# TensorE's side work in single pieces, one buffer each for delta and du, a ring of 12 slots, and a new order at the end of a batch

## The chip, the cores and the metric

The program runs on one core of a Trainium2 chip. The metric is the time of one execution on the device, in microseconds (us). All times below are in us unless marked ns. The engines are TensorE (PE, with its weight loads as PEld), VectorE (DVE), ScalarE (ACT), GpSimd (POOL) and SyncE (SP, which issues DMAs).

## The reference, cut to what matters

```python
# attention-like block: a selective state-space model; B=4, L=512, DM=256, DI=512, DS=16
x     = einsum('ed,bld->bel', in_proj_w, ctx)            # in_proj
u     = silu(causal_depthwise_conv(x, conv_w) + conv_b)
x_dbl = einsum('ke,bel->bkl', x_proj_w, u)               # 16 rows dt_lo, 16 rows B, 16 rows C
delta = softplus(einsum('er,brl->bel', dt_proj_w, dt_lo) + dt_proj_b)
A     = -exp(A_log)                                      # 512 x 16
state = state * exp(delta_t * A) + (delta_t * u_t) * B_t # for t in 0..511, 16 states per channel
y_t   = sum_n state * C_t
out   = (y + D * u) * silu(layernorm(x_in))              # added to x_in
# then, on layernorm(x): 8 experts of 512 -> 1024 -> 512, top 2 per token
gate_logits = einsum('bsd,de->bse', xln, gate_kernel)
```

## The kernel before

The program has two stages one after the other: `mamba_block` (the state-space part for four batches, ending with the gate logits) and `ffn_block` (the experts). The change touches only the first.

**Tiling.** A batch b (0 to 3) has 512 channels by 512 times, in two halves of 256 channels. For each half the 16 states n are worked through one by one; one state of one half is a *unit*, q = 32 b + s, with s = 0 to 31 the step in the batch. A unit holds 128 partitions by 1024 values and lives in one slot of `ring`. It passes through five operations:

- POOL `times_b` (L284): du times the broadcast row B, into the ring slot. POOL's code issues it four units (LEAD) ahead of its other work. It may not start before `acc` has emptied the slot, RING = 8 units back.
- ACT `exp_dA` (L368): two exponentials of 512, into three PSUM banks (SB = 3). It can therefore be three half units ahead of the scan, no more.
- DVE `scan` (L588): two scans of 512 along time.
- `times_c`: states times the broadcast row C. For n in (2, 5, 8, 11, 14) POOL does it (L293), from a DMA'd row; for the others DVE does it (L594) one step later than the scan, and the row comes from PE: `fill_c` (L733) writes the single PSUM bank Cb, and may only do so when the DVE product before it is done.
- PE `acc` (L753): 8 transposes that add the unit into yT, two units (LAG) later.

**Side work.** Between the units the engines prepare batch b + 1 and finish batch b - 1. Each engine's block is a loop over s with `if s == ...` lines, written out by hand, and each engine runs its own list in order. In order of use, for the next batch: PE `ctx_T`, `in_proj` (L772); ACT `tap`, DVE `conv` (L604), ACT `silu_u`; PE `x_proj` (L782), ACT `x_dbl` (L358), PE `dt_proj` (L790), ACT `dt_half` (L420, L421) and `soft` (L448, L452), DVE `loss` (L611), POOL `sub_loss` (L299), ACT `soft_log` (L456), POOL `add_ln` and `times_u` (L313), which gives the `du` that `times_b` needs. dt, `loss` and the rest are done in halves: half 0 of batch b + 1 in the second half of batch b, half 1 partly in batch b + 1. For the batch before: PE `zs_T` (of this batch's gate), DVE `drain_y` (L620), `stats_2`, POOL `rstd_2`, ACT `xln`, PE and ACT `gate_T`, PE `logits_of` (L814) and DVE `logit_copy` (L625). PE's side results go through two PSUM banks pp0 and pp1 in the order of the list USES. `logit_copy(b - 1)` stands after the loop over s, so DVE reaches it at the end of each of the batches 1 and 2, and for batch 3 after the last product.

## Time and profile before

| | us |
|---|---|
| median of 3 runs (lowest, highest) | 1291.56 (1291.31, 1293.41) |
| the profiled execution's own time | 1293.37 |
| its span in the trace | 1290.7 |
| PE busy | 1117.9 |
| DVE busy | 755.9 |
| POOL busy | 639.3 |
| ACT busy | 524.3 |

The first scan starts at 40.57 and the last product of the state-space part, `drain_y` of batch 3's second half, at 544.38; the rest of the span is its short tail and the experts, where PE is the chain. The first stage is where several engines pass small pieces to each other; busy shares over the whole span mix the two.

### The profile page before, as it was taken

The numbers are of one execution on the slowest core, as the hardware profiler recorded it, in microseconds if no ns is written. First come the engines' busy times: TensorE is split into PE (matmuls) and PEld (weight loads), VectorE is DVE, ScalarE is ACT, GpSimd is POOL, SyncE is SP. The second block draws the span as 40 slices with busy tenths as digits, with TensorE's granted clock in tenths as the row PEclk, the third lists the DMA queues.
The fourth block names the chain that finished last, engine by engine and source line by source line (L and its number), as shares of the span: only waits on it lengthen the run. The fifth ranks groups of instructions, "written<-read, shape, count | busy, mean of one in ns | idle before, by whom it ended". The sixth has DMA issues, their size and how long they took to land.

```text
span 1290.7 us, 19382 instructions
## 1 busy us (share of the span) xinstructions
PE 1117.9 (87%) x4940; PEld 836.3 (65%) x4940; DVE 755.9 (59%) x823; ACT 524.3 (41%) x706; POOL 639.3 (50%) x465
## 2 busy tenths in 40 slices
PE   6677778797788767738999999999999999999994
PEld 2344454465456545637788888888888888888883
DVE  5888999979987989656324343531532534324321
ACT  5955756665566554213223132421422323213210
POOL 0798999999989899304122232221321223212221
PEclk9677888878877767657999999999999999999997
DMA  6432232522432233064214353421531435215310
GB/s 208 142 104 92 84 112 76 174 85 87 129 110 90 82 112 109 0 250 174 99 41 164 106 179 113 165 105 43 179 104 35 171 108 179 105 41 171 106 47 19
DMA packets 65444, 145.08 MB, mean 112 GB/s; under 512 B 8654, under 2 KB 11214, under 8 KB 65408
## 3 DMA queue, kind: packets, MB, share of 16 engines
q1 hardware_dynamic: 56368, 116.34, 26.8%
q0 software_dynamic: 9040, 28.32, 6.7%
q8 instruction: 16, 0.26, 0.1%
q14 instruction: 20, 0.16, 0.0%
HBM read 320.53 MB, written 18.35 MB: 263 GB/s over the span
## 4 chain that ended last, share of the span: by engine, by line
PE 53%; DVE 2%; issue 0%; ACT 0%; POOL 0%; ACTq 0%; DVEq 0%; POOLq 0%
PE hp L1507 11%; PE hp L1506 11%; PE hp L1505 11%; PE yp L1505 5%; PE yp L1507 5%; PE yp L1506 5%; PE tp L1546 2%; PE xp L1499 1%; PE yp L1551 0%; DVE R L1343 0%; DVE S_tok L1339 0%; DVE S_w L1334 0%; DVE S_w L1447 0%; DVE S_w L1445 0%; DVE xT_lo L1402 0%
## 5 line engine op out<-in xcount | busy, mean ns | idle before, releaser
L284 POOL TENSOR_TENSOR ring<-du,bB 128x1024 f32<-128x1024 f32 x128 | 299.9, 2361 | 53.2 <-DVE du L654 36.7
L588 DVE TENSOR_TENSOR_SCAN ring<-dA,ring 128x512 f32<-128x512 f32 x256 | 296.0, 1205 | 15.4 <-ACT dA L368 9.9
L368 ACT ACTIVATE dA<-delta,Acol 128x512 f32<-128x512 f32 x256 | 172.3, 687 | 165.4 <-DVE ring L588 162.7
L1505 PE MATMUL hp<-w_hi,xT_hi 128*128 128x512 f32 x592 | 236.5, 399 | 2.1 <-DVE xT_lo L1402 2.1
L1507 PE MATMUL hp<-w_hi,xT_lo 128*128 128x512 f32 x592 | 236.2, 399 | 0.0
L1506 PE MATMUL hp<-w_lo,xT_hi 128*128 128x512 f32 x592 | 234.1, 396 | 0.0
L753 PEld LDWEIGHTS yT<-ident,ring 128*128 128x128 f32 x1024 | 146.7, 172 | 93.3 <-issue 76.2
L733 PE MATMUL Cb<-xdbl,ident 48*128 48x512 f32 x176 | 125.9, 802 | 91.8 <-DVE ring L594 91.8
L1144 POOL COPY out_index<-out_tab 128x1 uint32 x37 | 6.7, 181 | 356.5 <-DVE work L1409 356.5
L1423 DVE TENSOR_TENSOR work<-hp,work 128x512 f32<-128x512 f32 x74 | 51.1, 690 | 224.3 <-PE hp L1507 221.1
L753 PE MATMUL yT<-ident,ring 128*128 128x128 f32 x1024 | 172.8, 331 | 8.0 <-POOL ring L293 8.0
L1380 DVE TENSOR_TENSOR w_lo<-stage,w_hi 128x2048 fp32r<-128x2048 f32 x48 | 109.0, 2289 | 35.6 <-ACT w_hi L1190 35.4
L1505 PEld LDWEIGHTS hp<-w_hi,xT_hi 128*128 128x128 f32 x592 | 111.7, 189 | 28.0 <-DVE xT_lo L1402 1.8
L1506 PEld LDWEIGHTS hp<-w_lo,xT_hi 128*128 128x128 f32 x592 | 111.7, 189 | 26.9
L1507 PEld LDWEIGHTS hp<-w_hi,xT_lo 128*128 128x128 f32 x592 | 111.5, 188 | 26.1
L1505 PE MATMUL yp<-w_hi,iT_hi 128*128 128x512 f32 x296 | 121.8, 412 | 2.1 <-DVE iT_lo L1434 2.1
L594 DVE TENSOR_TENSOR ring<-Cb,ring 128x1024 f32<-128x1024 f32 x88 | 106.4, 1209 | 24.4 <-PE Cb L733 23.3
L1229 ACT CAST iT_hi<-tp 128x512 fp32r<-128x512 f32 x74 | 39.8, 590 | 194.5 <-PE tp L1546 194.5
L1507 PE MATMUL yp<-w_hi,iT_lo 128*128 128x512 f32 x296 | 117.3, 396 | 0.0
L1506 PE MATMUL yp<-w_lo,iT_hi 128*128 128x512 f32 x296 | 116.7, 394 | 0.0
L1409 DVE SCALAR_TENSOR_TENSOR work<-yp,wtab,work 128x512 f32<-128x512 f32 x37 | 27.8, 751 | 145.0 <-PE yp L1507 145.0
L733 PEld LDWEIGHTS Cb<-xdbl,ident 48*128 48x128 f32 x176 | 32.4, 229 | 122.1 <-DVE ring L594 66.8
(202 smaller groups left out, 1403.4 us busy)
## 6 DMA issues: line engine op xcount, KB each, us to landing
stage<-in_L_ffn_w_kernel_dram SPq DMA_DIRECT2D x160, 1024.0 KB
stage<-in_L_ffn_wo_kernel_dram SPq DMA_DIRECT2D x78, 1024.0 KB
bB<-bcs SPq DMA_DIRECT2D x64, 512.0 KB, 3.6
bC<-bcs SPq DMA_DIRECT2D x40, 256.0 KB, 4.4
xall<-in_x_dram SPq DMA_DIRECT2D x1, 4096.0 KB, 14.1
xln_dram<-xlnb SPq DMA_DIRECT2D x4, 1024.0 KB, 6.8
out_dram<-xall SPq DMA_DIRECT2D x4, 1024.0 KB, 8.9
ctx_rows<-in_ctx_dram SPq DMA_DIRECT2D x4, 512.0 KB, 6.0
```

The source lines that it names most:

```text
L284: g_.tensor_tensor(ring[:, q % RING, :].rearrange("p (e l) -> p e l", e=2), dub(b, h * 2 * L, 2 * L).rearrange("p (e l) -> p e l", e=2), B ...
L368: a_.activation(dA[r % SB][:, :], db(b, eb * L, L), ACT.Exp, scale=Acol[:, eb, n:n + 1]).then_inc(exp_done, 1)
L588: v_.tensor_tensor_scan(o, dA[r % SB][:, :], o, 0.0, ALU.mult, ALU.add).then_inc(scan_done, 1)
L594: v_.tensor_tensor(states, Cb[:, :].unsqueeze(1).to_broadcast([P, 2, L]), states, ALU.mult).then_inc(hc_dve, 1)
L733: t_.matmul(Cb[:, :], ident[0:rows, at:at + 1].to_broadcast([rows, P]), xdbl[:, b % 2, :], start=True, stop=True).then_inc(C_full, 1)
L753: last = t_.matmul(yT[:, t, e * P:(e + 1) * P], ring[:, q % RING, e * L + t * P:e * L + (t + 1) * P], ident[:, :], start=False, stop=(n == ...
L1229: s_.copy(iT_hi[:, 4 * h:4 * h + 4, :], tp[h][:, :].rearrange("p (k t) -> p k t", t=P)).then_inc(i_hi, 1)
L1380: v.tensor_tensor(w_lo[c][:, :, :], stage[c][:, :, :], w_hi[c][:, :, :].bitcast(fp32), ALU.subtract).then_inc(lo_done, 1)
L1423: v.tensor_tensor(inter[:, h, :], hp[2 + h][:, :], gated[:, h, :], ALU.mult).then_inc(inter_done, 1)
L1505: t_.matmul(bank[:, :], a_hi[:, k, :], b_hi[:, b, :], start=(start and k == ks[0]), stop=False)
L1506: t_.matmul(bank[:, :], a_hi[:, k, :], b_lo[:, b, :], start=False, stop=False)
L1507: last = t_.matmul(bank[:, :], a_lo[:, k, :], b_hi[:, b, :], start=False, stop=(stop and k == ks[-1]))
```

## The change

Five things are altered, none of which adds or removes an arithmetic instruction:

1. PE's side work is cut so that at most one piece (one bank of `ctx_T`, `zs_T`, `in_proj` or `gate_T`, half of `x_proj`, half of the logits) stands between two units.
2. `delta` and `du` have one buffer instead of two, so `dt_half` now waits for the exponentials and `times_u` of the batch before, and `loss` for the `times_b` of the batch before.
3. The ring has 12 slots instead of 8.
4. `dt_half(b + 1, 0)` and `soft` move from ACT's step 24 to 23 and `soft_log` from 27 to 26; PE's `dt_proj(b + 1, 0)` moves from 21 to 22.
5. `gate_T` of rows 2 and 3, the logits and `logit_copy` move ahead of `dt_proj(b + 1, 1)` and `dt_half(b + 1, 1)`: PE's gate from step 28 to 23 and 24, ACT's from 31 to 25, the logits from 31 to 26 and 27, DVE's copy from behind the loop to step 29, PE's second half of dt from 25 to 30, ACT's from 28 to 31.

```diff
--- before.py
+++ after.py
@@ -8,7 +8,7 @@
-RING = 8
+RING = 12
...
-        delta = sb("delta", [P, 2, EB * L])
-        du = sb("du", [P, 2, EB * L])
+        delta = sb("delta", [P, EB * L])
+        du = sb("du", [P, EB * L])
...
-            USES += [f"{n}.{b + 1}" for n in ("XP", "DT0", "DT1", "DT2", "DT3") if nxt]
+            USES += [f"{n}.{b + 1}" for n in ("XP", "DT0", "DT1") if nxt]
             USES += [f"{n}.{b - 1}" for n in ("G2", "G3", "LG") if rest]
+            USES += [f"{n}.{b + 1}" for n in ("DT2", "DT3") if nxt]
...
-                if b > 1:
-                    act.wait_ge(du_ready, g - 3)
+                if b > 0:
+                    act.wait_ge(du_ready, g - 1)
+                    act.wait_ge(exp_done, 2 * (q0(b - 1, i) + UPH))
...
                     if s == 21 and nxt:
                         x_dbl(b + 1)
-                    if s == 24 and nxt:
+                    if s == 23 and nxt:
                         dt_half(b + 1, 0)
                         soft(b + 1, 0)
-                    if s == 27 and nxt:
-                        soft_log(b + 1, 0)
-                    if s == 28 and nxt:
-                        dt_half(b + 1, 1)
-                    if s == 31 and rest:
+                    if s == 25 and rest:
                         gate_T(b - 1, 2)
                         gate_T(b - 1, 3)
+                    if s == 26 and nxt:
+                        soft_log(b + 1, 0)
+                    if s == 31 and nxt:
+                        dt_half(b + 1, 1)
...
-                if b > 1:
-                    dve.wait_ge(dbu_done, q0(b - 2, i) + UPH)
+                if b > 0:
+                    dve.wait_ge(dbu_done, q0(b - 1, i) + UPH)
...
                         loss(b + 1, 0)
-                if rest and nxt:
-                    logit_copy(b - 1)
+                    if s == 29 and rest:
+                        logit_copy(b - 1)
             if NU - 1 in NTH_DVE:
                 times_c(NU - 1)
-            logit_copy(NB - 2)
             drain_y(NB - 1, 1)
...
-            def x_proj(b):
+            def x_proj(b, ebs):
                 o, done = use(f"XP.{b}")
                 if b > 0:
                     pe.wait_ge(u_ready, b)
-                for eb in range(EB):
+                for eb in ebs:
                     if b == 0:
                         pe.wait_ge(u_part, eb + 1)
                     last = t_.matmul(o[0:DR + 2 * DS, :], xpT[:, eb, :], ub(b, eb * L, L), start=(eb == 0), stop=(eb == EB - 1))
-                last.then_inc(done, 1)
+                if eb == EB - 1:
+                    last.then_inc(done, 1)
...
-            def logits_of(b):
+            def logits_of(b, rows):
                 for i in (LB - 2, LB - 1):
                     k = USE[f"G{i}.{b}"]
                     pe.wait_ge(freed[k % 2], nth(k))
                 o, done = use(f"LG.{b}")
-                for i in range(LB):
+                for i in rows:
                     for d in range(DI // P):
                         last = t_.matmul(o[:, i * 8:(i + 1) * 8], gT[:, i, d * P:(d + 1) * P], gate[:, d, :], start=(d == 0), stop=(d == DI // P - 1))
-                last.then_inc(done, 1)
+                if i == LB - 1:
+                    last.then_inc(done, 1)
...
-                    if s == 0 and nxt:
-                        ctx_T(b + 1)
-                    if s == 3 and rest:
-                        zs_T(b, (0, 1))
-                    if s == 6 and rest:
-                        zs_T(b, (2, 3))
-                    if s == 4 and nxt and not rest:
-                        in_proj(b + 1, (0, 1))
-                    if s == 8 and nxt and rest:
-                        in_proj(b + 1, (0, 1))
-                    if s == 9 and not rest:
-                        zs_T(b, (0, 1))
-                    if s == 11 and not rest:
-                        zs_T(b, (2, 3))
-                    if s == 12 and nxt:
-                        in_proj(b + 1, (2, 3))
-                    if s == 16 and rest:
-                        gate_T(b - 1, 0)
-                        gate_T(b - 1, 1)
+                    if s in (0, 1) and nxt:
+                        ctx_T(b + 1, (s,))
+                    if s in (4, 5, 7, 8) and rest:
+                        zs_T(b, ((4, 5, 7, 8).index(s),))
+                    if s in (9, 10, 11, 12) and not rest:
+                        zs_T(b, (s - 9,))
+                    if s in ((9, 10) if rest else (4, 5)) and nxt:
+                        in_proj(b + 1, (s - (9 if rest else 4),))
+                    if s in (13, 14) and nxt:
+                        in_proj(b + 1, (s - 11,))
+                    if s in (16, 17) and rest:
+                        gate_T(b - 1, s - 16)
                     if s == 19 and nxt:
-                        x_proj(b + 1)
-                    if s == 21 and nxt:
+                        x_proj(b + 1, (0, 1))
+                    if s == 20 and nxt:
+                        x_proj(b + 1, (2, 3))
+                    if s == 22 and nxt:
                         dt_proj(b + 1, 0)
-                    if s == 25 and nxt:
+                    if s in (23, 24) and rest:
+                        gate_T(b - 1, s - 21)
+                    if s == 26 and rest:
+                        logits_of(b - 1, (0, 1))
+                    if s == 27 and rest:
+                        logits_of(b - 1, (2, 3))
+                    if s == 30 and nxt:
                         dt_proj(b + 1, 1)
-                    if s == 28 and rest:
-                        gate_T(b - 1, 2)
-                        gate_T(b - 1, 3)
-                    if s == 31 and rest:
-                        logits_of(b - 1)
```

The first place is PE around `x_proj` and `dt_proj` in the first of the batches that have all side work (batch 1, steps 18 to 23; u, xpT are `x_proj`, dtT is `dt_proj`, xlnb is the gate). Before:

```order
L733 MATMUL Cb<-xdbl,ident 128x512
L753 MATMUL yT<-ident,ring 128x128 x8
L782 MATMUL pp<-u,xpT 48x512 x4
L733 MATMUL Cb<-xdbl,ident 128x512
L753 MATMUL yT<-ident,ring 128x128 x16
L790 MATMUL pp<-xdbl,dtT 128x512 x2
L733 MATMUL Cb<-xdbl,ident 128x512
L753 MATMUL yT<-ident,ring 128x128 x8
```

and now:

```order
L734 MATMUL Cb<-xdbl,ident 128x512
L754 MATMUL yT<-ident,ring 128x128 x8
L783 MATMUL pp<-u,xpT 48x512 x2
L734 MATMUL Cb<-xdbl,ident 128x512
L754 MATMUL yT<-ident,ring 128x128 x8
L783 MATMUL pp<-u,xpT 48x512 x2
L754 MATMUL yT<-ident,ring 128x128 x8
L734 MATMUL Cb<-xdbl,ident 128x512
L754 MATMUL yT<-ident,ring 128x128 x8
L792 MATMUL pp<-xdbl,dtT 128x512 x2
L734 MATMUL Cb<-xdbl,ident 128x512
L754 MATMUL yT<-ident,ring 128x128 x8
```

The second half of `x_proj` now stands behind one more Cb fill and one more `acc`, and `dt_proj` behind another pair.

The second place is ACT in the same stretch (steps 21 to 28 and on). xdbl is `x_dbl`, the four with spy and delta are `dt_half`, the next two `soft`, dA are the exponentials of the units. Before:

```order
L358 ACTIVATE xdbl<-pp 48x512
L368 ACTIVATE dA<-delta,Acol 128x512 x6
L420 ACTIVATE spy<-pp,dtb 128x512
L421 ACTIVATE delta<-pp,dtb 128x512
L420 ACTIVATE spy<-pp,dtb 128x512
L421 ACTIVATE delta<-pp,dtb 128x512
L448 ACTIVATE spy<-spy 128x1024
L452 ACTIVATE spw<-spy 128x1024
L368 ACTIVATE dA<-delta,Acol 128x512 x6
L456 ACT_TABLE_LOAD
```

and now:

```order
L359 ACTIVATE xdbl<-pp 48x512
L369 ACTIVATE dA<-delta,Acol 128x512 x4
L422 ACTIVATE spy<-pp,dtb 128x512
L423 ACTIVATE delta<-pp,dtb 128x512
L422 ACTIVATE spy<-pp,dtb 128x512
L423 ACTIVATE delta<-pp,dtb 128x512
L450 ACTIVATE spy<-spy 128x1024
L454 ACTIVATE spw<-spy 128x1024
L369 ACTIVATE dA<-delta,Acol 128x512 x4
L359 ACTIVATE gT<-pp 128x512 x2
L369 ACTIVATE dA<-delta,Acol 128x512 x2
L458 ACT_TABLE_LOAD
```

There are four exponentials (two units) instead of six between `x_dbl` and `dt_half`.

The third place is DVE at the end of batch 1, from the product of unit 28 on. Before:

```order
L594 TENSOR_TENSOR ring<-Cb,ring 128x1024
L588 SCALAR_TENSOR_TENSOR ring<-dA,ring 128x512 x2
L594 TENSOR_TENSOR ring<-Cb,ring 128x1024
L588 SCALAR_TENSOR_TENSOR ring<-dA,ring 128x512 x2
L625 COPY logits<-pp 128x32
L588 SCALAR_TENSOR_TENSOR ring<-dA,ring 128x512 x2
```

and now:

```order
L596 TENSOR_TENSOR ring<-Cb,ring 128x1024
L627 COPY logits<-pp 128x32
L590 SCALAR_TENSOR_TENSOR ring<-dA,ring 128x512 x2
L596 TENSOR_TENSOR ring<-Cb,ring 128x1024
L590 SCALAR_TENSOR_TENSOR ring<-dA,ring 128x512 x4
```

The copy of the logits has moved two units forward.

## Rows read from the trace of the kernel before

**Rows 1.** Windows, batches 1 and 3: length, busy PE, PEld, DVE, ACT, POOL, clock, DMA, GB/s

```profile
163.47:291.23 127.76, 102.41 (x445) 65.57 (x444) 114.96 (x112) 80.32 (x114) 123.97 (x59) 0.81 0.37 114
...
418.97:533.64 114.67, 86.74 (x363) 57.61 (x364) 104.92 (x99) 58.33 (x84) 103.32 (x51) 0.72 0.26 85
```

**Rows 2.** DVE's waits from 40 to 545: waiter <- releaser: us in total, times, longest

```profile
DVE ring L594 <- PE Cb L733: 23.3, 17, 2.5
DVE logits L625 <- PE pp L814: 19.1, 3, 7.2
```

**Rows 3.** Timeline of DVE, batch 1, steps 22 to 31: start, us, what, [idle before]

```profile
253.15 4.56 DVE L588 TENSOR_TENSOR_SCAN ring<-dA,ring 128x512 f32<-128x512 f32 x4
...
258.73 2.33 DVE L588 TENSOR_TENSOR_SCAN ring<-dA,ring 128x512 f32<-128x512 f32 x2
...
262.65 2.34 DVE L588 TENSOR_TENSOR_SCAN ring<-dA,ring 128x512 f32<-128x512 f32 x2 [0.38 <-ACT dA L368]
264.91 1.20 DVE L611 SCALAR_TENSOR_TENSOR du<-spw,spy 128x1024 f32<-128x1024 f32 x1
...
291.12 0.19 DVE L625 COPY logits<-pp 128x32 f32<-128x32 f32 x1 [5.81 <-PE pp L814]
```

**Rows 4.** Timeline of PE, batch 1, steps 19 to 24

```profile
245.13 1.12 PE L733 MATMUL Cb<-xdbl,ident 48*128 48x512 f32 x2
246.19 1.09 PE L753 MATMUL yT<-ident,ring 128*128 128x128 f32 x8
247.21 3.63 PE L782 MATMUL pp<-u,xpT 128*48 128x512 f32 x8
...
253.72 1.98 PE L790 MATMUL pp<-xdbl,dtT 16*128 16x512 f32 x4
...
258.87 2.07 PE L733 MATMUL Cb<-xdbl,ident 48*128 48x512 f32 x2 [1.09 <-DVE ring L594]
```

**Rows 5.** Timeline of ACT, batch 1, steps 21 to 24

```profile
250.88 0.59 ACT L358 ACTIVATE xdbl<-pp 48x512 f32<-48x512 f32 x1 [3.50 <-PE pp L782]
...
257.25 0.67 ACT L420 ACTIVATE spy<-pp,dtb 128x512 f32<-128x512 f32 x1
...
261.88 2.72 ACT L368 ACTIVATE dA<-delta,Acol 128x512 f32<-128x512 f32 x4
```

**Rows 6.** Timeline of POOL, batch 1, from `sub_loss` to the next first `times_b`

```profile
266.19 2.35 POOL L299 TENSOR_TENSOR delta<-delta,du 128x1024 f32<-128x1024 f32 x1 [2.27 <-DVE du L611]
...
282.57 2.35 POOL L284 TENSOR_TENSOR ring<-du,bB 128x1024 f32<-128x1024 f32 x1
```

**Rows 7.** Timeline of DVE, batch 1, the second `conv`

```profile
225.83 4.01 DVE L604 SCALAR_TENSOR_TENSOR u<-pp,convw,u 128x511 f32<-128x511 f32 x6
```

**Rows 8.** The end of batch 3: timelines of DVE and of PE

```profile
540.87 0.19 DVE L625 COPY logits<-pp 128x32 f32<-128x32 f32 x1 [7.23 <-PE pp L814]
544.38 1.22 DVE L620 TENSOR_TENSOR g<-yT,zsT 128x1024 f32<-128x1024 f32 x1 [3.31 <-PE yT L753]
...
534.00 6.83 PE L814 MATMUL pp<-gate,gT 128*128 128x8 f32 x32
540.69 3.65 PE L753 MATMUL yT<-ident,ring 128*128 128x128 f32 x16
```

**Rows 9.** One line, L611 (`loss`): ns min/median/max, and first and last start

```profile
L611 DVE SCALAR_TENSOR_TENSOR du<-spw,spy x8: 1199/1200/3377, 32.4 to 433.8; 128x1024 f32<-128x1024 f32 x8
```

**Rows 10.** Timelines of DVE and POOL, batch 1, step 3, the long `loss`; POOL's waits on ring slots

```profile
179.34 3.38 DVE L611 SCALAR_TENSOR_TENSOR du<-spw,spy 128x1024 f32<-128x1024 f32 x1
...
179.28 2.35 POOL L293 TENSOR_TENSOR ring<-ring,bC 128x1024 f32<-128x1024 f32 x1
181.59 5.63 POOL L284 TENSOR_TENSOR ring<-du,bB 128x1024 f32<-128x1024 f32 x2
...
POOL ring L284 <- PE yT L753: 16.0, 9, 3.5
```

**Rows 11.** Timeline of ACT, batch 1, step 13, `xln`, which waits for POOL's `rstd_2`

```profile
216.61 2.93 ACT L480 ACTIVATE xlnb<-xall,nm,rs 128x512 f32<-128x512 f32 x4 [0.41 <-POOL nm L264]
```

12 lines of the change are left out of this document (6 added, 6 removed).

## The prediction

> **What bounds the kernel now.** I read the windows by batch first. Batch 1 lasts 127.76 with DVE busy 114.96 and POOL 123.97, and batch 3 114.67 with DVE 104.92 [rows 1]: no engine is idle for long, so what counts is how far each runs ahead of the next. DVE is where the units come together, so I read its waits next: 23.3 for Cb in 17 waits, 19.1 for the logits in 3 [rows 2]. The logits' waits are 5.81 at the end of batch 1 [rows 3], 7.23 at the end of batch 3 [rows 8], and so 6.1 for batch 2. Then the timelines around the moved pieces. The reader is to see in them that ACT is fed by PE just in time: `x_dbl` starts at 250.88 after a wait of 3.50 for `x_proj` [rows 5], which ends at 250.84 [rows 4], and the scan of unit 22 starts at 253.15 [rows 3], about 1.1 after its exponential, whose 0.69 ends near 252.1. What comes later on PE than now reaches DVE almost in full, because only three half units of exponentials can be ready.
>
> **Units of cost.** At 2.4 GHz a Cb fill takes 1.1 and an `acc` 1.1 (1.12 and 1.09); half of `x_proj` is 1.8 (half of 3.63) and a `dt_proj` bank 1.0 (half of 1.98) [rows 4]. At 1.2 GHz a fill takes 2.07 [rows 4] and an `acc` 1.8 (half of 3.65) [rows 8]. A scan pair is 2.25 (4.56 for two pairs) [rows 3]; a DVE product adds 1.1, taken from the same spacing. The logits of a batch take 6.83 [rows 8], so a half is 3.4, or about 2.6 where the clock is high (an estimate from the fill's ratio, softened because their cost is weight loads).
>
> **Term 1: x_proj in halves, dt half 0 one unit earlier on ACT: +3.3 in each of batches 0, 1, 2, so +9.9.** In batch 1 the first half ends at 249.0; the fill of unit 20 waits for the product before it (about 248.9) and ends at 250.1, `acc` at 251.2, and the second half at 253.0 instead of 250.84. `x_dbl` (0.59) and the exponential (0.69) follow: scan 22 at 254.4, not 253.15, though the Cb wait before it is gone. Then PE does `acc`, fill, `acc` (3.3) and the first dt bank: 257.3. ACT needs from the start of `dt_half` to the end of the next exponential 257.25 to 261.88, and 0.69: 5.3 [rows 5]. So the exponential of unit 24 is there at 262.6, while DVE wants it at 254.4 + 4.5 + 1.1 = 260.1: it idles 2.5. Now scan 24 starts at 258.73 and scan 25, after one more product, at 262.65 with 0.38 idle [rows 3]. After the change scan 25 starts at 262.6 + 2.25 + 1.1 = 266.0: 3.3 late. Bounds: 0 if all of it hides, 9 if the clock is low (fills, `acc` and matmuls double, +5.7).
>
> **Term 2: the end of batches 1 and 2: -1.7 and -2.0.** From the end of `loss` (266.11) to scan 0 of the next batch (291.23) it is 25.1 now [rows 3]. POOL's own chain from `loss` to its next `times_b`, 266.19 to 284.92, is 18.7 [rows 6], a floor. With both logits halves in front of the fill of unit 28, and `dt_proj` behind `acc(28)`, PE's work after the product of unit 25 is fill, acc, half, acc, half, fill, acc, fill, acc, acc, two dt banks: at 2.4 GHz about 16, then ACT's two last operations and an exponential (2.1), and 3.4 from `loss` to that product: 21.2 to 21.5. The other way to it is from now's own run: there PE got through its list, logits last, at 291.1. The new list in front of dt lacks the last unit's fill and `acc` (2.2) and the gate (1.0), has the two dt banks (2.0) and idles about 1.5 less, so it ends near 288.4, and 2.1 behind that the exponential is 24.4 after `loss`. Between 21.5 and 24.4, both from rows, I take 23.4, nearer to the second because the granted clock was 0.81 there, some 40% of the time at the low level [rows 1]. So not 5.8 and 6.1 come back but 1.7 and 2.0; bounds -3.8 and, with the whole list at 1.2 GHz (26 instead of 16), +6 each. What is late next is `dt_half(b + 1, 1)`, behind which the next batch's exponentials are queued.
>
> **Term 3: batch 0's end, +1.1.** No logits there, but `dt_proj(1)` waits on PE behind `acc(27)`, which waits for POOL's `times_c`; in POOL's chain [rows 6] that is 14 after `loss`, so dt arrives at 18.1 and the exponential at 20.2, against 19.1 now (25.1 - 5.8 - 0.2 of batch 1, which is alike).
>
> **Term 4: in_proj banks 2 and 3 a unit later, +2.7.** After the product of unit 12 PE needs fill, acc, 1.8, acc, 1.8 = 6.9, and ACT's tap 0.8: 7.7. `conv` (at 225.83 now [rows 7]) wants that bank 6.3 after the product: +1.4 in batches 1 and 2, 0 in batch 0, where a Cb wait of about the same size goes. Bounds 0 and 3.5 each.
>
> **Term 5: the first halves, +2.0.** `zs_T` and the first `in_proj` banks also come one or two units later to ACT. In batch 1 POOL covers this: scan 14 needs `xln` (at 216.61, waiting for POOL's `rstd_2` [rows 11]), and POOL is busy all the time. In batch 2, where POOL now starts ahead thanks to the logits wait, I count 2.0, bounds 0 and 5.
>
> **Term 6: gate_T in halves, -2.1.** It shortens one Cb wait in each of batches 1 and 2, mean wait 23.3/17 = 1.4 [rows 2]; 0 to -2.8, and I take -2.1.
>
> **Term 7: ring of 12, single buffers, 0.** POOL waits 16.0 in 9 times for a ring slot [rows 10]. But DVE has only to wait for POOL at the start of batch 0; a POOL that is not stopped there waits for `loss` instead, as it does for 2.27 now [rows 6]. The new waits of `dt_half`, `loss` on `exp_done` and `dbu_done` are for units at least 8 steps old, except for exponential 31 just before `dt_half(1)`, 0.2. Behind `dt_half` stand only exponentials, counted in terms 1 and 2. Batch 3 starts with less POOL lead (+1.0) and has shorter waits for Cb (-0.9).
>
> **Term 8: the end of batch 3, -5.4.** From the end of the last product (533.6) to `drain_y` (544.38) it is 10.7 [rows 8]. With the logits done earlier only the last `acc` is left, 1.3: -9.4. But at 1.2 GHz PE has no room to hide 6.8 of logits: they would then hold up the products of units 28 to 31 by nearly as much. By the same 40% I take -5.4; bounds -10 and -1.
>
> **Sum.** 9.9 - 3.7 + 1.1 + 2.7 + 2.0 - 2.1 + 0.1 - 5.4 = +4.6. The profiled execution took 1293.37 (span 1290.7), so it becomes 1298.0; the median of the runs is 1.8 lower, which gives 1296.2. The tail and the experts, the same instructions, keep their time.
>
> **The rule weighed against the trace.** One `loss` of the 8 took 3377 ns, the median is 1200 [rows 9]. It started at 179.34, 0.06 after a POOL product, and POOL's next pair took 5.63 instead of 4.68 [rows 10]: 2.2 lost on DVE and 1.0 on POOL. Others that I read start while POOL waits. The Trainium skill, SBUF — State Buffer, section "SBUF: two separate sides", says that VectorE instructions with two SBUF inputs and GpSimd instructions hold a shared port pair as an exclusive lock for the whole instruction. The trace agrees with it in this one place. By that rule the larger ring has a price: POOL, no longer stopped, is in the middle of an operation when `loss` of batches 2 and 3 comes. By the row it would be 2.2 twice, which half fits in term 5's 2.0 for batch 2 and is under POOL's cover in batch 3; by the rule without cover the sum is 2.4 more, 1298.6.
>
> **The rivals.** (A) The pieces do what their cut suggests, and the later feeding is hidden or the denser PE stays at 2.4 GHz: terms 1, 3, 4, 5 shrink to 3 in all, terms 2 and 8 reach -7.3 and -9.4, and with term 6 it is -16: 1276 (to 1285 if only half comes). For it: 23.3 of Cb waits [rows 2] are to be had. Against: `x_dbl`'s 3.50 of waiting [rows 5] at 2.4 GHz. This is the rival on the other side; it decides where terms 1, 3, 4, 5 (15.7) fall below 8.5. Chance 0.32. (B) PE at 1.2 GHz through units 19 to 31: term 1 to +9 each in two of three batches, term 2 to +1.7: +12 over the forecast, 1308; chance 0.12. For it: 0.72 of clock in batch 3 [rows 1]. (C) POOL becomes the bound: it is busy 123.97 of 127.76 in batch 1 and 103.32 of 114.67 in batch 3 [rows 1], so 3.8 are to be had in each of batches 1 and 2 and 11.4 in batch 3. That leaves A possible as it stands and only caps it, at 1266 with the 9.4 of the end. (D) Both sides cancel, the moved waits being equal to the old ones: 1291.5, chance 0.12.
>
> **How the numbers follow.** The forecast, from 1292 to 1301, has 0.44. A measurement here can tell about 0.2%, 2.6. Faster by more than that: A nearly whole and a little of D and the forecast's low side, 0.34. Within: 0.20 (D and the low side of the forecast). Slower: 0.46. The range 1278 to 1307 leaves out the far ends of A and B.
>
> **What would show it.** Right: DVE idle before scan 24 of batches 0 to 2 for ACT, about 2.5 each, and `x_dbl` waiting over 5; no logits wait; a wait for Cb at unit 28 of batches 1 to 3; `drain_y` of batch 3 within 2 to 5 of the last product; POOL's ring waits gone, its waits for `loss` longer. Wrong: if scan 24 does not wait, or if `x_proj`'s second half ends before the scan of unit 21 does; or if the granted clock in batches 1 to 3 rises above 0.9.

## The result and the profile after

The changed kernel takes 1341.1 us (median of 3 runs, 1339.7 to 1341.6) against 1291.56: 1.0377 times before, with a 95% interval of 1.0353 to 1.0401. The prediction was 1296.2, with 1307 as its upper end. The profiled execution has a span of 1338.5, 47.8 more than before.

The windows by batch, from the first scan of one batch to that of the next (the last one to `drain_y`); columns as in [rows 1]:

```profile
38.80:170.70 131.90, 93.88 (x366) 56.99 (x366) 108.30 (x101) 80.42 (x112) 114.29 (x55) 0.75 0.28 89
170.70:317.60 146.90, 113.60 (x438) 72.24 (x436) 113.60 (x112) 79.93 (x114) 126.64 (x61) 0.73 0.31 100
317.60:466.70 149.10, 113.47 (x432) 70.17 (x431) 115.63 (x112) 80.00 (x114) 119.93 (x58) 0.72 0.28 93
466.70:592.20 125.50, 99.19 (x420) 68.47 (x418) 106.33 (x100) 59.30 (x86) 98.52 (x48) 0.69 0.21 73
```

Batch 1 is 19.1 longer than in [rows 1], and not for more work on DVE or POOL: DVE is busy 113.60 (114.96 before), POOL 126.64 (123.97 before, with two instructions fewer). PE does the same work too and is busy 11.2 longer in batch 1, at 0.73 instead of 0.81 of the clock. DVE's waits from 40 to 600, beside [rows 2]:

```profile
DVE ring L590 <- ACT dA L369: 56.6, 24, 6.1
DVE ring L596 <- PE Cb L734: 29.7, 19, 6.4
DVE u L606 <- ACT u L377: 18.5, 8, 3.9
DVE g L622 <- PE yT L754: 3.9, 5, 1.5
```

The logits' 19.1 are gone. In their place exponentials are waited for 56.6 (9.9 before), taps of `conv` 18.5 (none before), and Cb 29.7. All of DVE's waits make 109.6 now and 63.6 before, and this difference of 46.0 is nearly all of the 47.8 of the span. Where they are, in batch 1: DVE's timeline, with the first `conv` (its second instruction waits), scans 22 and 24, the product of unit 28 and the next batch's first scan:

```profile
224.17 3.37 DVE L606 SCALAR_TENSOR_TENSOR u<-pp,convw,u 128x511 f32<-128x511 f32 x5 [3.89 <-ACT u L377]
...
273.12 4.57 DVE L590 TENSOR_TENSOR_SCAN ring<-dA,ring 128x512 f32<-128x512 f32 x4 [2.85 <-ACT dA L369]
...
281.51 2.34 DVE L590 TENSOR_TENSOR_SCAN ring<-dA,ring 128x512 f32<-128x512 f32 x2 [2.71 <-ACT dA L369]
...
305.99 1.23 DVE L596 TENSOR_TENSOR ring<-Cb,ring 128x1024 f32<-128x1024 f32 x1 [6.06 <-PE Cb L734]
...
317.56 2.34 DVE L590 TENSOR_TENSOR_SCAN ring<-dA,ring 128x512 f32<-128x512 f32 x2 [4.20 <-ACT dA L369]
```

And PE's timeline for two of them: the `in_proj` bank in front of that instruction of `conv` (bank 1 of 0 to 3), and the list from the first half of the logits on:

```profile
219.69 3.62 PE L773 MATMUL pp<-ctxT,wT 128*128 128x512 f32 x4
...
295.44 3.42 PE L816 MATMUL pp<-gate,gT 128*128 128x8 f32 x16
298.72 1.95 PE L754 MATMUL yT<-ident,ring 128*128 128x128 f32 x8
300.46 3.42 PE L816 MATMUL pp<-gate,gT 128*128 128x8 f32 x16
303.81 2.07 PE L734 MATMUL Cb<-xdbl,ident 48*128 48x512 f32 x2
305.81 1.97 PE L754 MATMUL yT<-ident,ring 128*128 128x128 f32 x8
```

Everything in this list has the durations of 1.2 GHz: the fill 2.07 as the slow one in [rows 4], each half of the logits 3.42. A fill took 1.12 and an `acc` 1.09 in [rows 4] where the level was 2.4 GHz. The product of unit 28 can't start before the fill at 303.81 is through.

### The profile page after: what moved, and what is told of

Read it like the earlier page. It is cut to its first block, busy times and chain, and to the rows that moved or that the text cites. A ratio compares the mean times of both kernels' runs of the same rounds, so it can differ in the third digit from the quotient of the medians.

```text
span 1338.5 us, 19411 instructions
## 1 busy us (share of the span) xinstructions
PE 1143.3 (85%) x4940; PEld 849.5 (63%) x4940; DVE 758.7 (57%) x823; ACT 525.2 (39%) x706; POOL 640.6 (48%) x465
## 4 chain that ended last, share of the span: by engine, by line
PE 50%; DVE 2%; DMA 0%; issue 0%; POOL 0%; ACT 0%; POOLq 0%; DVEq 0%
PE hp L1506 10%; PE hp L1505 10%; PE hp L1504 10%; PE yp L1504 5%; PE yp L1506 5%; PE yp L1505 5%; PE tp L1545 2%; PE xp L1498 1%; PE yp L1550 0%; DVE R L1342 0%; DMA work<-out_dram,acc_index 0%; DMA out_dram<-work,out_index 0%; DVE S_tok L1338 0%; DVE S_w L1333 0%; DVE S_w L1446 0%
## 5 line engine op out<-in xcount | busy, mean ns | idle before, releaser
L590 DVE TENSOR_TENSOR_SCAN ring<-dA,ring 128x512 f32<-128x512 f32 x256 | 296.1, 1203 | 58.1 <-ACT dA L369 56.6
L734 PE MATMUL Cb<-xdbl,ident 48*128 48x512 f32 x176 | 134.7, 855 | 121.8 <-DVE ring L596 121.8
L754 PEld LDWEIGHTS yT<-ident,ring 128*128 128x128 f32 x1024 | 155.8, 180 | 104.0 <-issue 96.9
L754 PE MATMUL yT<-ident,ring 128*128 128x128 f32 x1024 | 186.3, 344 | 3.5 <-POOL ring L294 3.5
L294 POOL TENSOR_TENSOR ring<-ring,bC 128x1024 f32<-128x1024 f32 x40 | 95.1, 2378 | 76.0 <-DVE ring L590 76.0
L596 DVE TENSOR_TENSOR ring<-Cb,ring 128x1024 f32<-128x1024 f32 x88 | 106.3, 1208 | 30.4 <-PE Cb L734 29.7
```

The source lines that it names most:

```text
L294: g_.tensor_tensor(states, states, C, ALU.mult).then_inc(hc_pool, 1)
L590: v_.tensor_tensor_scan(o, dA[r % SB][:, :], o, 0.0, ALU.mult, ALU.add).then_inc(scan_done, 1)
L596: v_.tensor_tensor(states, Cb[:, :].unsqueeze(1).to_broadcast([P, 2, L]), states, ALU.mult).then_inc(hc_dve, 1)
L734: t_.matmul(Cb[:, :], ident[0:rows, at:at + 1].to_broadcast([rows, P]), xdbl[:, b % 2, :], start=True, stop=True).then_inc(C_full, 1)
L754: last = t_.matmul(yT[:, t, e * P:(e + 1) * P], ring[:, q % RING, e * L + t * P:e * L + (t + 1) * P], ident[:, :], start=False, stop=(n == ...
```

## The experiments

Seventeen kernels, in the order of what they tell. Ratios are to the kernel before on the same chip in the same sitting. In these sittings that kernel ran between 1291.7 and 1314.6, and its median was 1296.4, 1302.5, 1296.7, 1302.2 and 1297.4 (1291.56 beside the changed kernel). So the intervals reach some 0.3 to 0.9% to either side, and two ratios of different sittings can differ by half a percent for the kernel before alone. Where that matters, times and the spans of the profiled executions stand beside them; a span is one execution only.

**1. Is it the buffers and the ring?** The changed kernel with the old buffers, their old waits and the old ring; order and pieces stay:

```diff
-RING = 12
+RING = 8
...
-        delta = sb("delta", [P, EB * L])
-        du = sb("du", [P, EB * L])
+        delta = sb("delta", [P, 2, EB * L])
+        du = sb("du", [P, 2, EB * L])
```

> The changed kernel with its order and pieces kept, but delta and du with two buffers each, the waits of before on them, and 8 ring slots. Theory F (feeding: pieces of side work reach ScalarE later than its fixed place, and VectorE waits for exponentials queued behind them): nothing comes back, 1341 within 4 us; ScalarE waits of the scans stay near 56.6 us and conv's waits for tap near 18.5 us. Theory W (the single buffers' new waits, or a ring that lets GpSimd run into VectorE's loss): most of the 48 us comes back, below 1310 us.

1348.5, ratio 1.0388 (1.0311 to 1.0465). Nothing comes back: ring and single buffers don't cost the 3.8%.

**2. The late pieces alone.** The kernel before with `ctx_T`, `zs_T`, `in_proj`, gates 0 and 1 and `x_proj` in pieces at the change's steps; dt, gates 2 and 3 and the logits as before:

```diff
-                    if s == 8 and nxt and rest:
-                        in_proj(b + 1, (0, 1))
...
-                    if s == 12 and nxt:
-                        in_proj(b + 1, (2, 3))
...
+                    if s in (4, 5, 7, 8) and rest:
+                        zs_T(b, ((4, 5, 7, 8).index(s),))
...
+                    if s in ((9, 10) if rest else (4, 5)) and nxt:
+                        in_proj(b + 1, (s - (9 if rest else 4),))
+                    if s in (13, 14) and nxt:
+                        in_proj(b + 1, (s - 11,))
```

> The kernel before, with only TensorE's pieces of ctx_T, zs_T, in_proj, gate_T 0 and 1 and x_proj at the steps of the changed kernel; dt, gate 2 and 3, logits, buffers and ring as before. Theory F: conv's waits for tap (18.5 us in the changed kernel) and the waits of scans 7, 9, 10, 12 and 22 appear here too, some 25 to 35 us longer than before, 1317 to 1327 us. Theory O (the order at the end of a batch, dt behind gate and logits, is what costs): at most 1300 us. Theory W: 1285 to 1295 us.

1323.4 (two executions, 1317.9 and 1328.9), ratio 1.0194 (1.0105 to 1.0284): half of the loss, with conv waits of 18.9 like the changed kernel's.

**3. The rest without them.** The changed kernel with PE's side work up to step 19 whole and at the old steps (the diff of 2 the other way round):

> The changed kernel, but TensorE's side work up to step 19 (ctx_T, zs_T, in_proj, gate_T 0 and 1, x_proj) whole and at the steps of before; single buffers, ring of 12, the new order from step 22 on kept. Theory F: the complement of the run with late pieces alone, so some 25 to 35 us less than 1341, 1306 to 1316 us; scan 24's wait and the Cb wait at unit 28 stay. Theory O: 1330 to 1341 us. Theory W: about 1341 us.

1316.5 (two executions), ratio 1.0142 (1.0062 to 1.0221). The two halves, +1.9% and +1.4%, make 3.4% and, with these intervals, are about the change's 3.8%. By span they are +24.4 and +20.5 of 47.8.

**4. Pieces that aren't late.** The changed kernel with each pair's last piece at the step of the old whole, `x_proj` whole at 19:

```diff
-                    if s in ((9, 10) if rest else (4, 5)) and nxt:
-                        in_proj(b + 1, (s - (9 if rest else 4),))
-                    if s in (13, 14) and nxt:
-                        in_proj(b + 1, (s - 11,))
+                    if s in ((7, 8) if rest else (3, 4)) and nxt:
+                        in_proj(b + 1, (s - (7 if rest else 3),))
+                    if s in (11, 12) and nxt:
+                        in_proj(b + 1, (s - 9,))
```

> The changed kernel, but the pieces of zs_T, in_proj and of gates 0 and 1 put so that each pair's LAST piece stands at the step where the whole stood before (the first a unit sooner), and x_proj whole at step 19. All that follows step 20 stays as in the changed kernel. Late feeding: in the change every pair began where it used to begin and ended one or two units later, and that is what the waits of conv (18.5), of scans 7, 9 and 10 and of scan 22 are; here they go, and the time is that of the run with this work whole at the old steps, 1.014 times before, 1308 to 1316. Rival, the cutting itself costs (each piece is its own wait for a bank and a fresh start of the engine): the conv waits go but waits for Cb and for exponentials come in their place, over 1.025 times before. Second rival, pieces do help when they aren't late: 5 or more below the whole ones, under 1.010.

1320.2, ratio 1.0118 (1.0074 to 1.0163); the conv waits are gone. It equals experiment 3 within the intervals: no cost of the cut is seen, the lateness costs. Cb is waited for 45.5 here, 29.7 in the changed kernel, but 41.2 in experiment 3 too, so these waits are not of the pieces.

**5. Are pieces worth something, then?** The same early pieces on the kernel before, all from step 19 on as before:

> The kernel before with ctx_T, zs_T, in_proj and gates 0 and 1 in pieces, each pair's last piece at the step where the whole stood; x_proj, both halves of dt, gates 2 and 3 and the logits as before. It asks whether the cutting is worth anything when it isn't late. On the changed kernel the same edit removed the conv waits and gave 29 of the 48 back, and it was no better than whole work at the old steps (1.012 against 1.014). If cutting is worth nothing: within 0.3% of before, since what a Cb wait loses in one unit another one gains. Rival A's idea, that pieces free the Cb fills: the waits at units 17 and 20 (0.9 to 2.1 each in batches 1 and 2) go and nothing comes: 0.995. Rival, the cut costs by a lower granted clock, as PE's idle time is spread: 1.005 or more.

1295.1, ratio 0.9970 (0.9943 to 0.9997). 0.3% at most, which the interval hardly tells from nothing.

**6. in_proj late, alone.** The kernel before with

```diff
-                    if s == 8 and nxt and rest:
-                        in_proj(b + 1, (0, 1))
+                    if s in (9, 10) and nxt and rest:
+                        in_proj(b + 1, (s - 9,))
...
-                    if s == 12 and nxt:
-                        in_proj(b + 1, (2, 3))
+                    if s in (13, 14) and nxt:
+                        in_proj(b + 1, (s - 11,))
```

> The kernel before with one pair of edits: in_proj's banks 0, 1 at steps 9 and 10 (not both at 8) of batches 1 and 2, and banks 2, 3 at 13 and 14 (not both at 12) of batches 0, 1 and 2; all else as before. The prediction had +2.7 for banks 2 and 3 (1.4 in each of batches 1 and 2) and a part of the +2.0 of the first halves: +3.7, 1.003. Late feeding as the changed kernel's trace shows it: conv waits 3.9 and 4.5 in batch 1, 3.3 and 4.1 in batch 2 and 2.7 in batch 0, 18.5 in all, and DVE has nothing to take them up: +10 to +16, 1.008 to 1.012, with the taps on ACT waiting 6 or more for the bank. If conv waits show but the time is within 3 of before, the waits are taken up by POOL's slack, and the +27 of the run with all late pieces came from zs_T or x_proj.

1314.6, ratio 1.0103 (1.0069 to 1.0137). Its waits of DVE, 40 to 570:

```profile
DVE ring L594 <- PE Cb L733: 25.3, 19, 2.6
DVE logits L625 <- PE pp L814: 25.2, 3, 9.0
DVE u L604 <- ACT u L376: 12.0, 7, 2.1
```

Against [rows 2]: 12.0 for taps is new, Cb is 2.0 more, and the logits are waited for 6.1 longer, not shorter. The late bank is not made up for at the batch's end.

**7. zs_T late, alone.** The kernel before with `zs_T` in pieces at 4, 5, 7, 8 (9 to 12 in batch 0):

> The kernel before with zs_T alone in pieces at the change's steps (4, 5, 7, 8 in batches 1 to 3, 9 to 12 in batch 0). All late pieces together gave 1.019, in_proj's alone 1.010; ctx_T and gates 0 and 1 are one step at most. By addition zs_T has what is left, with x_proj's halves at nothing: 1.005 to 1.009, with scans 7, 9 and 10 waiting for exponentials queued on ACT behind the copies of zs_T (1.8, 0.8 and 2.1 in the changed kernel's batches 1 and 2). By the prediction's term 5 all first halves are worth +2.0, so zs_T about 1.001. Rival: the waits show, and the logits wait at the end of batches 1 and 2 shrinks by as much: within 0.3% of before.

1297.4, ratio 0.9966 (0.9940 to 0.9992). Exponentials are waited for 26.4 instead of 9.9, but the logits 14.2 instead of 19.1, Cb 17.3 instead of 23.3 and POOL 2.1 instead of 5.6: for the most part hidden. The profiled execution is less clear than the ratio: its span is 5.2 more than before, with batch 1 4.3 longer and the other three 0.2 shorter together.

**8. Term 1 alone.** The kernel before with `x_proj` in halves at 19 and 20, ACT's `soft_log` at 26 and

```diff
-                    if s == 21 and nxt:
+                    if s == 22 and nxt:
                         dt_proj(b + 1, 0)
...
-                    if s == 24 and nxt:
+                    if s == 23 and nxt:
                         dt_half(b + 1, 0)
```

> The kernel before with term 1 of the prediction alone: x_proj in halves behind the fills of units 19 and 20, dt_proj for half 0 at step 22, and its dt_half and soft on ACT at step 23, soft_log at 26. Term 1 was sized at +3.3 in each of three batches, +9.9, with DVE idle some 2.5 before scan 24. If it is that: 1.0077 times before. Rival, undersized as the other terms were: in the change scan 22 waited 2.85 and scan 24 2.71, both for exponentials, so 5.6 in each batch less the 1.2 to 1.6 of other waits that they replace, +12 to +13, 1.010. Rival, swallowed: with the logits wait at the end of batches 1 and 2 and half 1 of dt where it was, DVE's lateness of 3 in the middle is taken up by POOL's slack and the end waits get shorter by as much: 1.000 to 1.003.

1295.6, ratio 0.9960 (0.9932 to 0.9987); span 1291.0, against 1290.7 before. In its profile scan 24 waits 2.69 to 2.71, as forecast, scan 22 2.09 to 2.85, and batches 0, 1, 2 are 3.2, 1.8 and 1.6 longer than before: +6.6. But batch 3, in which the edit issues nothing, is 6.7 shorter (experiment 10 says by what).

**9. The order of the batch's end alone.** The kernel before with

```diff
-                    if s == 25 and nxt:
+                    if s in (23, 24) and rest:
+                        gate_T(b - 1, s - 21)
+                    if s == 26 and rest:
+                        logits_of(b - 1, (0, 1))
+                    if s == 27 and rest:
+                        logits_of(b - 1, (2, 3))
+                    if s == 30 and nxt:
                         dt_proj(b + 1, 1)
```

ACT has gates 2 and 3 at step 26 and `dt_half(b + 1, 1)` at 31, DVE its copy at 29.

> The kernel before with the order of the batch's end alone (terms 2, 3 and 8 of the prediction): gate_T of rows 2 and 3 at steps 23 and 24, logits in halves at 26 and 27, logit_copy at step 29, dt_proj for half 1 at step 30 and its dt_half at 31; half 0 of dt and x_proj as before. The prediction put these terms at -3.7, +1.1 and -5.4: -8.0, 0.994. Rival from the changed kernel's trace: the product of unit 28 waits 6.1 to 6.4 for Cb in each of batches 1 to 3, scan 0 then waits 4 to 6 for the exponential behind dt_half, and only batch 3's end gives some 9 back: sum of these waits (19 + 10 + 2.6) against logits, yT and Cb waits of before (19.1 + 2 + about 4), so +5 to +12, 1.004 to 1.009. With the +20 of the run that had both this and the early half 0, this run and the one with term 1 alone should add to about +20.

1292.0, ratio 0.9949 (0.9918 to 0.9979); span 1290.8. Batches 0 to 3 change by +1.7, +1.0, +5.4 and -9.3.

**10. Both together.** Parts 8 and 9 on the kernel before, with its buffers and ring:

> The kernel before with term 1 (x_proj in halves at 19 and 20, half 0 of dt a step sooner on ACT) and the order of the batch's end (gates 23, 24, logits in halves 26, 27, dt_proj for half 1 at 30) together; two buffers, ring of 8, the work to step 16 as before. Alone the two gave 0.996 and 0.995; the changed kernel with its work to step 19 as before, which holds both, gave 1.014. If the two lose only together, by TensorE standing at 1.2 GHz from unit 24 of each batch to its end (scan 0 waits 6.1 and the product of unit 28 6.4, where the run with the end alone had 2.2 and 4.0 in batch 1): 1.012 to 1.018. If the loss of the other run comes from single buffers and the ring of 12: 0.990 to 0.994, the product of the two.

1314.2, ratio 1.0106 (1.0062 to 1.0151); span 1311.4. Neither part loses alone (the gains of 0.4 and 0.5% in the ratios don't show in the spans), and together they lose 1%. In batches 0 to 2 the two parts had cost 6.6 and 8.1 alone; together they cost 22.0 (+5.4, +7.7 and +8.8). And batch 3, which part 9 made 9.3 shorter, has its old length.

What differs there is the clock. Windows over batch 3 from scan 25 to `drain_y`; part 9 alone:

```profile
517.86:543.74 25.88, 24.83 (x134) 18.39 (x132) 21.76 (x21) 9.82 (x14) 16.80 (x8) 0.78 0.00 1
```

both parts:

```profile
529.67:564.73 35.06, 32.41 (x134) 24.55 (x132) 21.98 (x21) 10.51 (x15) 16.78 (x8) 0.60 0.00 1
```

PE, DVE and POOL have the same work in both; 0.78 of the clock in the one, 0.60 in the other, and 9.2 us. The logits halves take 1.85 and 2.56 in the first; in the second, each takes 3.42. Such a difference also comes without any difference in batch 3's program, on part 8 against the kernel before. From scan 25 on, before and part 8:

```profile
510.11:544.38 34.27, 29.52 (x134) 22.63 (x132) 21.75 (x22) 9.90 (x14) 16.36 (x8) 0.70 0.00 1
...
517.55:544.58 27.03, 25.98 (x134) 19.00 (x132) 21.77 (x21) 9.90 (x14) 16.78 (x8) 0.75 0.00 0
```

The means of the clock are close, but the level is low under the logits before, which take 6.83 [rows 8], and high in part 8, where they take 3.64. There its 6.7 lie.

Between part 9 alone and the joint run there is one difference in batch 3's program. Like the change, the joint run has gates 2 and 3 on ACT at step 25; part 9 alone had them at 26. ACT's timeline in the joint run:

```profile
531.27 0.60 ACT L359 ACTIVATE gT<-pp 128x512 f32<-128x512 f32 x1 [3.12 <-PE pp L805]
533.84 0.60 ACT L359 ACTIVATE gT<-pp 128x512 f32<-128x512 f32 x1 [1.96 <-PE pp L805]
534.33 2.74 ACT L369 ACTIVATE dA<-delta,Acol 128x512 f32<-128x512 f32 x4
```

ACT stands 3.12 and 1.96 for transposes that PE has just begun, scan 26 waits 3.1 for the exponential behind them, PE idles 2.6 for DVE and its next fill takes 2.07, as at 1.2 GHz.

**11. That one step taken back.** Experiment 10's kernel, and the changed kernel, with

```diff
-                    if s == 25 and rest:
+                    if s == 26 and rest:
                         gate_T(b - 1, 2)
                         gate_T(b - 1, 3)
```

> The kernel before with both parts (1.0106), but ACT takes gates 2 and 3 at step 26, as in the run of the batch's end alone, and not at 25. In batch 3 it is then the same program as that run, which ended that batch in 25.9 from scan 25 where the joint run took 35.1. In the joint run ACT waited 3.1 and 2.0 for those transposes at step 25, scan 26 waited 3.1 for the exponential behind them, PE stood idle 2.6 for DVE and came back at 1.2 GHz, with the logits halves at 3.42 each. If this step alone makes the difference: batch 3's end back at about 26 and the time at 1.003 to 1.005. If the clock goes down by what came before, batch 3's end stays at 33 to 35 and the ratio at 1.008 to 1.012.

> The changed kernel with gates 2 and 3 on ACT at step 26 instead of 25, nothing else. If this step lets batch 3's end go at 2.4 GHz: 9 less there, 1.030 to 1.032, the rest of the 3.8% staying, as it comes from in_proj, from scans 22 and 24 and from the ends of batches 1 and 2. If the clock is down for other reasons: 1.035 to 1.039, the wait at scan 26 alone (3.1) being gone.

The joint run becomes 1305.3, ratio 1.0072 (1.0040 to 1.0103), and its batch 3 from scan 25 is again what part 9 alone had, to the hundredth:

```profile
529.28:555.16 25.88, 24.82 (x134) 18.37 (x132) 21.77 (x22) 9.81 (x14) 16.77 (x8) 0.78 0.00 1
```

The changed kernel becomes 1333.4, ratio 1.0269 (1.0235 to 1.0302). That is 1.1% under 1.0377, but the two ratios are of different sittings; the time is 7.7 (0.6%) under the changed kernel's. Its batch 3 from scan 25, with step 25 and with 26:

```profile
557.11:592.16 35.05, 32.38 (x134) 24.55 (x132) 21.97 (x21) 10.51 (x15) 15.23 (x7) 0.60 0.00 1
...
572.33:600.21 27.88, 27.48 (x134) 21.03 (x132) 21.88 (x21) 9.74 (x14) 13.84 (x6) 0.70 0.00 1
```

So one ACT step holds 8 to 14 of the change's 49.5, a sixth to over a quarter. All profiles sort by it: this stretch takes 25.9 to 27.9 in the four kernels that have the new order with ACT's gates at 26 (experiments 9, 11 twice and 12), and 32.7 to 35.1 in the five with 25 (the changed kernel, experiments 1, 3, 4 and 10). How the step acts is shown in part only. The wait of scan 26, 3.1, follows from it. But in the joint run the low level was there before: in experiments 10 and 11 PE does the same up to the first of these transposes; then the level is 1.00 from 530.3 to 540.5 with step 26, while with step 25 it stays at 0.50 to 534.1, with PE busy all the time, and falls again at 537.5, while PE stands. Why it rose earlier in the one is not shown.

**12. Buffers and ring kept, half 0 of dt as before.** Experiment 3's kernel with `dt_proj(b + 1, 0)` at 21, its ACT steps at 24 and 27, and gates 2 and 3 on ACT at 26:

> The changed kernel with its side work to step 19 whole and at the old steps (1.014), and half 0 of dt at the old steps too (dt_proj 21, dt_half and soft 24, soft_log 27, gates 2 and 3 on ACT 26): what is left of the change is the order of the batch's end, the ring of 12 and the single buffers. By the theory that half 0 and the end lose only together: 0.993 to 0.998, as the end alone had, with a granted clock of 0.8 at the end of batch 0 and dt_proj at 1.98. If single buffers or the ring cost: 1.005 to 1.014, with scan 0 waiting 5 to 6 in batch 1.

1298.1, ratio 1.0001 (0.9966 to 1.0036). With half 0 and ACT's gates at 26 the 1.4% are gone, though the ring of 12 and the single buffers stay. Its profiled execution was 12.0 longer than its median, for a reason of its own (last section).

**13. Can PE be kept at 2.4 GHz?** One more matmul (zeros, added to yT) behind `acc` in steps without side work, on the changed kernel and, also in step 20, on experiment 3's:

```diff
+                    if s in (15, 18, 21, 25, 28, 29) and q >= LAG and UNIT[q - LAG][2] < UPH - 1:
+                        t_.matmul(yT[:, 0:2, :], zw[:, :], xdbl[:, b % 2, :], start=False, stop=False, skip_group_check=True)
```

> The changed kernel with one more matmul (zeros times 512 columns into yT, added to it, so that the sums stay as they are) behind acc at steps 15, 18, 21, 25, 28 and 29, where PE has no side work: 1.0 each at 2.4 GHz, 2.0 at 1.2 GHz, 23 of them. It asks whether the granted clock follows what PE does in its idle time. If it does and rises to over 0.9 in the second half of the batches, the logits halves (3.42), the fills (2.07) and acc (1.97) of units 26 to 31 fall to about half, the Cb wait of 6.1 at unit 28 falls to about 2 and scan 0's to 2: 1.015 to 1.025 times before instead of 1.038. Rival: the clock does not follow, PE has 46 more to do at 1.2 GHz, of which half is on the way: 1.045 to 1.06.

> The same extra matmuls at steps 15, 18, 20, 21, 25, 28 and 29, on the changed kernel with its side work to step 19 whole and at the old steps (1.014). There PE stood at 0.50 from about step 22 of batch 0 to the end of the batch, 20 of it without a pause, while the run with the batch's end order alone had 1.00 in most of the same stretch, with dt_proj at 1.98 instead of 3.78 and scan 0 of batch 1 waiting 2.2 instead of 6.1. If the clock is what the two parts lose together (each alone cost nothing, 0.996 and 0.995), a rise of the clock here brings the time to 0.995 to 1.005. If the clock rises and the time does not fall, the two parts' loss is one of order, not of clock. If the clock stays at 0.50 the run tells nothing of that and costs 1.02 or more.

1373.9, ratio 1.0594 (1.0550 to 1.0638), and 1336.7, ratio 1.0293 (1.0240 to 1.0347). The rival of both held. Windows of the second at the end of batch 0 and of batch 1:

```profile
160.00:170.00 10.00, 10.00 (x26) 5.29 (x25) 6.52 (x6) 1.09 (x2) 9.87 (x6) 0.50 0.13 52
170.00:176.90 6.90, 6.90 (x13) 2.52 (x12) 0.00 (x0) 3.29 (x6) 6.90 (x4) 0.50 0.41 114
...
300.00:310.00 10.00, 10.00 (x26) 5.60 (x27) 4.23 (x5) 0.69 (x1) 9.87 (x5) 0.50 0.21 70
310.00:320.00 10.00, 10.00 (x22) 4.45 (x20) 2.80 (x3) 2.50 (x4) 10.00 (x5) 0.50 0.34 112
```

PE has not a moment's pause and is granted 0.50. This extra work did not bring the clock back; it only came on top.

**14. Logits waited for later.** The kernel before with `logit_copy(b - 2)` on DVE at step 1 of the next batch, and the last logits behind the last `acc`:

```diff
+                    if s == 1 and b > 1:
+                        logit_copy(b - 2)
...
-                if rest and nxt:
-                    logit_copy(b - 1)
...
-                    if s == 31 and rest:
+                    if s == 31 and rest and nxt:
                         logits_of(b - 1)
             for q in range(NU - LAG, NU):
                 acc(q)
+            logits_of(NB - 2)
```

> The kernel before, with only this: VectorE copies the logits of batches 0 and 1 at step 1 of the batch after next instead of waiting at the batch's end, and the logits of batch 2 are computed behind the last acc, their copy behind the last layer norm's chain. If the waits for the logits (19.1 us before) are really VectorE's, the two inner ones give back 4 us each (the fill of the next unit still stands behind the logits on TensorE) and the end 6.8 us: 1275 to 1281 us. If they only hide others (GpSimd, ScalarE catch up in them), the inner ones give back nothing: 1284 to 1286 us.

1284.1, ratio 0.9894 (0.9835 to 0.9954): faster than both kernels. Batches 1, 2 and 3 are 6.0, 3.8 and 1.6 shorter than before. The waits of 19.1 for the logits are gone, and Cb is waited for 30.6 instead of 23.3 (2.3 and 5.5 of it at the first products of batches 2 and 3).

**15. The same with halves, a batch on.** Logits in halves behind `acc` in steps 0 and 1 of the next batch, `ctx_T` behind them, the copy at step 2:

> The kernel before, with the logits of batch b not whole behind the last fill of batch b+1 but in two halves behind acc in steps 0 and 1 of batch b+2, ctx_T behind them at step 2, logit_copy on DVE at step 2, and the last logits behind the last acc. The run with the logits whole at the batch's end and only their copy later gave 0.989 and kept Cb waits of 2.3 and 5.5 at the product of unit 0 of batches 2 and 3. If a half costs 1.8 to 3.4 on PE in units where DVE has only scans and a product, those two waits fall by about half: 0.985 to 0.989. Rival: PE runs at 1.2 GHz there (0.5 granted through the first stretch of the batch), a half takes 3.4, each of two products waits 2 to 3, and nothing is won on the whole: 0.989 to 0.993.

1289.4, ratio 0.9934 (0.9908 to 0.9961), not better than 14: a product waits 4.77 for Cb and `logit_copy` behind it 3.82 in batch 2, and as long in batch 3.

## Why the prediction was wrong

In short: the places of the waits were right, the prices were not. Three steps failed. Late `in_proj` banks were priced at 2.4 GHz and as covered by POOL, some 4; alone they cost 18.6 of span. The end of batches 1 and 2 was to give back 3.7; alone it costs 6.4. And ACT's gates at step 25 had no term; they cost some 9 of span. Besides, the terms were added as if the clock stayed as it was. Nearly all of the prediction's signs of being right came (a wait before scan 24, `x_dbl` waiting 6.83, no logits wait, the wait at unit 28, POOL's ring waits gone) with a time 45 above it: they told of places, not of sizes. Two did not come: `drain_y` of batch 3 starts 1.5 after the last product, not 2 to 5, and POOL's waits for `loss` are no longer (6.4 against 6.8).

Point by point, by its own terms.

- **Term 1** (+9.9): place and mechanism right. `x_dbl` waits 6.83, scan 24 waits 2.71. Its size was +6.6 in experiment 8, in batches 0 to 2. Scan 22 was put 1.2 later and waited 2.85.
- **Terms 4 and 5** (+2.7 and +2.0): this is half of what failed. The second `conv` was put at 1.4 late in batches 1 and 2; it waits 4.5 and 4.1, and the first one 3.9 and 3.3. `in_proj` late, alone, costs 1.0% (+13), where some 4 were forecast. By span it is 18.6, of which batches 1 and 2 have 11.1 and 8.9. Two steps of the working failed. The banks were counted at 1.8, but in front of each `conv` of batch 1 stands one of 3.62. And "in batch 1 POOL covers this" did not hold for `in_proj`. For `zs_T` the ratio says that it did (experiment 7); its profiled execution has batch 1 4.3 longer. Batch 0's second `conv`, put at 0, waits 2.7.
- **Terms 2, 3 and 8** (-1.7 and -2.0, +1.1, -5.4): alone, the batch's end gave +1.7, +1.0, +5.4 and -9.3 by batches, and a ratio of 0.9949 where these terms make 0.9938. So terms 3 and 8 had the right sign and place, and term 2 was too favourable by 10: with most of the list at 1.2 GHz (0.66 and 0.63 from scan 25 on) nothing comes back there. In the changed kernel batch 3 gave nothing back (125.5 against 125.4), and the waits at unit 28 were 6.1 to 6.4.
- **A step that has no term.** Gates 2 and 3 go from ACT's step 31 to 25, right behind their transposes on PE; the working priced them on PE alone. "Behind `dt_half` stand only exponentials" was checked, what stands behind `gate_T` wasn't. Experiment 11 prices it at 8 (by the times) to 14 (by the ratios), and at 9.2 of span in the joint run.
- **The sum** adds terms that don't add. Each was priced with the clock of [rows 1] kept (0.81, "some 40% of the time at the low level"), while from scan 25 on batches 1 and 2 of the changed kernel ran at 0.66 and 0.59. Parts 8 and 9 are 0.9960 and 0.9949 alone, and 1.0072 (1.0040 to 1.0103) together even with the ACT step at 26: batch 3's end can be shortened once, and in batches 0 to 2 they cost 21.8 together, not 14.7. Rival B (PE at 1.2 GHz through units 19 to 31) is nearest to what happened; it had 0.12, and its +12 over the forecast was too little. By its own terms it is +16.8 (5.7 twice, and 5.4 from -3.7 to +1.7), 1313, and it left terms 4 and 8 as they were. (Rival C's cap is 1263 by its own terms, not 1266; nothing hangs on it.)
- **Term 7** (0): right in size, by experiments 1 and 12. POOL's waits for ring slots, 16.0 in [rows 10], are gone. They did not turn into waits for `loss`, as the term had it, but into waits for scans (`ring L294 <- DVE ring L590`, 76.0 in 17).
- **Term 6** (-2.1) was not run by itself. Experiment 5 holds it beside other pieces, at 0.9970; its interval can't tell 2.1 from nothing.
- **The rule on the shared port**: the runs gave it much more weight than the sum did (last section), but not for this difference. As it said, `loss` of batches 2 and 3 is long in the changed kernel, 3.27 and 2.50, but that of batch 1 is 1.29 instead of 3.38 [rows 9]: in all 3.5 above 1.20 each, and 2.2 before.

By spans, the late pieces (experiment 2) are +24.4 and the joint run of experiment 10 +20.7: 45.1 of the 47.8. In the first, `in_proj` late is +18.6 alone and `zs_T` late +5.2 alone. In the second, term 1 is +6.6 and the ends of batches 0 to 2 +8.1, as alone; 7.3 more appear in batches 0 to 2 only when both are there; batch 3's end is -9.3 and the ACT step, which takes them back, +9.2. Each is the span of one execution, and executions of one kernel differ by as much as some of these. That the 7.3 are the clock is argued from the granted levels, not shown by a run of its own. Open too is why the clock is low in one order and not in the other: the traces show when it was granted, not why.

## What to carry to other kernels

When an engine feeds another just in time, the end of its last piece counts: cut a block so that the last piece stays where the whole was, or don't cut. Price each edit at both levels of TensorE's clock, and don't add terms that were priced with the clock held: run the parts alone and together, since here two edits that cost nothing alone made a loss of 1%. Of a moved step, look on every engine at what queues behind it: ACT's copies of two gates a step too soon cost 0.6 to 1.1%, and DVE's copies of the logits, put off so that nothing waits for them, gained 1% (experiment 14).
